# From block 4 to 14 the output's projection of two chunks as seven products of quarters

## The chip, the cores and the metric

The kernel runs on one core of one Trainium2 chip. The metric is the device time of one execution in microseconds (us). Five engines of the core are named as in the profile: PE (matmuls), DVE (VectorE), ACT (ScalarE), POOL (GpSimd) and SP, which here only issues transfers.

## The reference

`x` has 4 sequences of 1024 tokens with 1024 channels. What is computed, cut to its core:

```python
xn = layernorm(x)
h = rmsnorm(xn, qkv_norm_w); q, k, v = split(h @ ternary(qkv_w).T)      # 16 heads of 64
for each chunk of 128 tokens:                                            # S is carried on
    o = D ** -0.5 * ((q k^T * mask) v + (q * lam_t) S)
    S = lam_T * S + (k * lam_rev)^T v
s = rmsnorm(rmsnorm(o, norm_w, 1e-6), proj_norm_w, eps) @ ternary(proj_w).T
g = silu(xn @ ternary(ffn_weight).T + ffn_bias)
out = x + s * g
```

`ternary` rounds a weight matrix to -1, 0 and 1 times one scale, so that the weights are held in 8 bits (fp8) and are exact. The activations are held as two 16-bit parts, a high and a low one (`o_hi`, `o_lo`), and each product with weights is done twice, once for each part, into the same PSUM bank.

## The kernel before

Tokens are taken in chunks of T = 128; two chunks (c = 0, 1) are one block, and there are NB = 16 blocks, four to a sequence. Each engine has its own program, a list of instructions in an order written out by hand, and the engines meet only at semaphores. PE's matmuls write into four PSUM banks of 512 columns, `ring`, which are given out in turn by the list `ring_uses`: the use with number n takes bank n modulo 4, and `free_bank` makes PE wait until the use with number n - 4 has been read out. Four more banks, `att_ps`, serve the attention.

In block i (from block 3 on) PE does in this order:

- four groups of q and k (`project_qk`), with the two small matmuls of the norm of chunk 1 of the block before (`output_scale`, `spread_gamma`) between them;
- k and v of both chunks by `k_product` and `v_product`, and between them the projection of chunk 1 of the block before, `project_out(i - 1, 1, half)`. Here k, v and the ffn are already seven products of quarters instead of eight (Winograd's form of Strassen's scheme: rows are the two chunks, columns the two halves of the channels). A product has 4 x 2 matmuls of 512 columns. The names a11 to a22 are quarters of the activations, S1 to S4 their sums, w11 to w22 quarters of the weights, T1 to T4 their sums; products that share a part of the result share a bank;
- the attention of chunk 0 with products of the ffn between its steps, the same for chunk 1, and then the projection of chunk 0, `project_out(i, 0, half)`.

`project_out` is 8 x 2 matmuls of 512 columns into one bank, four times in a block. DVE makes the operand: `weight_o`, `scale_o` (times the norm's factor, which comes out of PE's `spread_gamma`), ACT's `high_o` rounds it to `o_hi`, DVE's `split_o` subtracts to `o_lo`. DVE's `gate_out` multiplies the bank by the gate, and POOL's `add_out` adds x; SP stores.

In the same stretch DVE prepares the next block: `norm_stats`, `sum_b` and `low_b_sum` for k and v, `low_part` and `sum_y` for the ffn, `add_k` and `add_v`, which add a bank to k or v, and `centre`, which takes mean and deviation off the turned x. POOL's `decay_q` scales q for the carried state; for chunk 0 of a block it is left out where a sequence begins (blocks 0, 4, 8, 12).

Of the kernel before, what the change touches and what calls it, by code (L numbers as in the profile page):

```python
# [36 lines left out]
def program(nc, x, qkv_w, proj_w, decay, ffn_w, ffn_b, norm_cols, x_turned, out):  # L37
# [17 lines left out]
    with ExitStack() as ctx:  # L55
# [16 lines left out]
        xt = sb("xt", [P, 4, C])  # L72
# [21 lines left out]
        arena = sb("arena", [P, ARENA])  # L94
# [28 lines left out]
        k_decay = arena[:, QL_OFF + C:QL_OFF + 2 * C]  # L123
        state = arena[:, ST_OFF:SM_OFF].rearrange("p (k r e) -> p k r e", k=2, r=PR)
# [3 lines left out]
        sq_sum = sb("sq_sum", [P, CHUNKS, 2, T])  # L128
# [6 lines left out]
        s_tok = sb("s_tok", [P, H])  # L135
        s_pair = sb("s_pair", [P, PR])
        cols = sb("cols", [P, 3, NCB])
        peak = sb("peak", [P, 10])
        mean_sq = sb("mean_sq", [P, P])
        neg_magic = sb("neg_magic", [P, 1])  # L140
        to_end = sb("to_end", [P, 1])
        mean_w = sb("mean_w", [P, 1])
        halves = sb("halves", [P, 4])
        wsum = sb("wsum", [P, 5 * NCB])
        wtot = sb("wtot", [P, 4])
# [3 lines left out]
        og = sb("og", [P, 2, 4])  # L149
        diag = sb("diag", [P, CHUNKS, T])  # L150
        sum_cols = sb("sum_cols", [P, PR, 1])
# [5 lines left out]
        diff = sq_sum[:, 0, 0, :]  # L157
        t_row = sq_sum[:, 0, 1, :]
# [60 lines left out]
        s_add_last = sem("last_out_added")  # L219

# [21 lines left out]
        def gate_of(i):  # L242
            return gate_odd if i == 1 else gate_even

# [36 lines left out]
        BY_TOKENS = 3  # L281
        PRODUCTS = ("p1", "p6", "p2", "p7", "p4", "p5", "p3")
# [213 lines left out]
        for i in range(BY_TOKENS, NB):  # L496
            ring_uses += [("qk", i, j) for j in range(CPH)]

            ring_uses += [("proj", i - 1, 1, 0), ("k product", i, "p1"), ("k product", i, "p5"), ("proj", i - 1, 1, 1)]
            ring_uses.append(("k product", i, "p6"))  # L500
# [3 lines left out]
            ring_uses += [("proj", i, 0, 0), ("proj", i, 0, 1)]  # L504
# [22 lines left out]
        def emptied(use):  # L527
# [14 lines left out]
            if kind == "v product":  # L542
                by = {"p1": (s_v, 2 * CHUNKS * HALF + of_pair(use[1], 0)), "p5": (s_vsum, of_pair(use[1], 0)),
                      "p6": (s_v, 2 * CHUNKS * HALF + of_pair(use[1], 1))}
                return by[use[2]]
            if kind == "product":
                return s_z, of_z(use[1], *{"p1": (0, 0), "p6": (1, 0), "p5": (0, 1)}[use[2]])
# [12 lines left out]
            return s_m, of_half(*use[1:])  # L560
# [36 lines left out]
        def tensor_program(pe):  # L597
# [61 lines left out]
            def product(i, name):  # L659
# [18 lines left out]
                for j in range(CPH):  # L678
                    if name == "p4" and i >= BY_TOKENS and j == CPH // 2:
# [1759 lines left out]
```

## Time and profile before

| | |
|---|---|
| median of 3 runs | 1329.47 us (1328.97 to 1329.55) |
| the profiled execution, its own time | 1328.99 us |
| its span in the profile | 1327.8 us |
| PE busy | 1304.3 us, 98% |
| DVE, ACT, POOL busy | 917.4, 581.9, 555.3 us (69%, 44%, 42%) |
| share of PE in the chain that ended last | 95% |

The span leaves out what lies around the program on the device, 1.2 us here. A busy share is that of the whole span; what each engine does in one block is read from a window as long as a block. A matmul is shown with its whole way through the array, so that rows of PE overlap, and the distance from start to start is what one costs.

### The profile page before, as it was taken

The page shows a single profiled execution, that of the slowest core. Times are in us where ns is not written, and L with a number is a line of the kernel's source. Part 1 is how long each engine was busy: PE and PEld are TensorE (multiplying, and loading weights), DVE is VectorE, ACT ScalarE, POOL GpSimd, SP SyncE. Part 2 cuts the span into 40 slices and gives each one's busy share as a digit, 9 for nine tenths or more (in the row PEclk, how much of TensorE's full clock was granted, in tenths as well). Part 3 has the DMA queues.
Part 4 walks back from the last instruction along what each step waited for, and adds up shares of the span by engine and source line. Part 5 has one row for each costly group of instructions (what it writes and reads, how often), then busy time and mean ns, then how long its engine had stood idle before and what let it go on. Part 6 is the DMA issues. An engine that isn't in the chain of part 4 may idle for free.

```text
span 1327.8 us, 25789 instructions
## 1 busy us (share of the span) xinstructions
PE 1304.3 (98%) x10351; PEld 835.2 (63%) x10351; DVE 917.4 (69%) x1457; ACT 581.9 (44%) x1139; POOL 555.3 (42%) x532
## 2 busy tenths in 40 slices
PE   4999999999999999999999999999999999999998
PEld 2577767674666656566674656657566575656655
DVE  7887466786666857667575776857667685766735
ACT  5884144343534544344353434544444453434521
POOL 1432876842433435335331543435334342533332
PEclk9999999999999999999999999999999999999999
DMA  9622201203021030300303021030300203020000
GB/s 363 240 96 65 72 33 42 94 17 120 1 66 71 17 119 18 116 5 17 120 17 120 2 100 37 17 120 17 117 4 20 116 17 120 1 88 18 33 33 33
DMA packets 33432, 90.32 MB, mean 68 GB/s; under 512 B 10529, under 2 KB 10785, under 8 KB 33314
## 3 DMA queue, kind: packets, MB, share of 16 engines
q1 hardware_dynamic: 33024, 88.65, 18.9%
q8 instruction: 83, 1.36, 0.4%
q14 instruction: 35, 0.29, 0.1%
q10 hardware_dynamic: 290, 0.02, 0.0%
HBM read 71.85 MB, written 16.81 MB: 67 GB/s over the span
## 4 chain that ended last, share of the span: by engine, by line
PE 95%; ACT 2%; DVE 1%; DMA 1%; issue 1%; SPq 0%; POOL 0%; ACTq 0%; DVEq 0%; POOLq 0%
PE ring L749 20%; PE ring L879 16%; PE ring L682 13%; PE ring L708 13%; PE ring L734 12%; PE att_ps L786 4%; PE att_ps L836 4%; PE att_ps L832 4%; PE ring L798 2%; PE att_ps L813 2%; PE ring L761 1%; PE ring L655 1%; DMA raw<-in_ffn_w 1%; ACT junk L1698 1%; PE ring L893 1%
## 5 line engine op out<-in xcount | busy, mean ns | idle before, releaser
L749 PE MATMUL ring<-b_lo,qkv_q 128*128 128x256 f16 x1216 | 268.2, 272 | 0.0
L749 PE MATMUL ring<-b_hi,qkv_q 128*128 128x256 f16 x1216 | 268.2, 273 | 0.0
L879 PE MATMUL ring<-proj_q,o_hi 128*128 128x512 fp8e4 x496 | 188.1, 379 | 1.0 <-DVE o_lo L1423 1.0
L879 PE MATMUL ring<-proj_q,o_lo 128*128 128x512 fp8e4 x496 | 188.0, 379 | 0.0
L2140 POOL TENSOR_TENSOR gate_even<-gate_even,bias 128x512 f32<-128x512 f32 x14 | 19.8, 1414 | 275.6 <-ACT gate_even L1817 275.4
L749 PEld LDWEIGHTS ring<-b_hi,qkv_q 128*128 128x128 fp8e4 x1216 | 120.2, 99 | 15.6
L749 PEld LDWEIGHTS ring<-b_lo,qkv_q 128*128 128x128 fp8e4 x1216 | 119.0, 98 | 15.7
L2180 POOL TENSOR_TENSOR sq<-sq,cols 128x1024 f32<-128x1024 f32 x29 | 55.0, 1897 | 157.6 <-DVE b_lo L1255 149.4
L2206 POOL TENSOR_TENSOR xt<-xt,gate_even 128x512 f32<-128x512 f32 x58 | 85.7, 1487 | 81.0 <-DVE gate_even L1440 80.8
L1857 ACT ACTIVATE arena<-ring,wscale 128x512 f32<-128x512 f32 x64 | 44.0, 687 | 128.5 <-PE ring L749 128.5
L1841 ACT ACTIVATE gate_even<-gate_even 128x512 f32<-128x512 f32 x60 | 37.3, 625 | 134.5 <-DVE gate_even L1286 134.5
L836 PE MATMUL att_ps<-arena 128*64 128x128 f32 x1024 | 95.0, 273 | 0.0
L1352 DVE TENSOR_TENSOR arena<-att_ps,mask 128x512 f32<-128x512 f32 x128 | 79.5, 684 | 14.4 <-PE att_ps L786 14.4
L832 PE MATMUL att_ps<-arena 128*64 128x128 f32 x896 | 88.5, 276 | 0.0
L879 PEld LDWEIGHTS ring<-proj_q,o_hi 128*128 128x128 f16 x496 | 48.6, 98 | 58.5 <-DVE o_lo L1423 1.1
L879 PEld LDWEIGHTS ring<-proj_q,o_lo 128*128 128x128 f16 x496 | 48.5, 98 | 56.0
L1286 DVE SCALAR_TENSOR_TENSOR gate_even<-ring,ln,gate_even 128x512 f32<-128x512 f32 x70 | 52.5, 750 | 39.7 <-PE ring L682 39.7
L1440 DVE SCALAR_TENSOR_TENSOR gate_even<-ring,wscale,gate_even 128x512 f32<-128x512 f32 x58 | 43.4, 748 | 45.0 <-PE ring L879 44.6
L2155 POOL TENSOR_TENSOR arena<-arena,lam_q 128x512 f32<-128x512 f32 x56 | 72.8, 1319 | 2.6 <-PE att_ps L836 2.6
L1802 ACT ACTIVATE gate_odd<-ring,wscale 128x512 f32<-128x512 f32 x26 | 17.9, 688 | 122.7 <-PE ring L734 122.7
L2076 POOL TENSOR_TENSOR ln<-ln,halves 128x3 f32<-128x3 f32 x32 | 37.5, 1171 | 80.2 <-DVE ln L1143 79.2
L786 PEld LDWEIGHTS att_ps<-arena 64*128 64x128 f32 x1024 | 59.7, 188 | 13.8 <-issue 13.8
(255 smaller groups left out, 3190.7 us busy)
## 6 DMA issues: line engine op xcount, KB each, us to landing
xt<-in_x SPq DMA_DIRECT2D x62, 512.0 KB, 8.1
out<-xt SPq DMA_DIRECT2D x31, 512.0 KB, 2.7
raw<-in_qkv_w SPq DMA_DIRECT2D x24, 512.0 KB, 15.7
y<-in_x_turned SPq DMA_DIRECT2D x14, 512.0 KB, 6.8
y_odd<-in_x_turned SPq DMA_DIRECT2D x14, 512.0 KB, 7.4
raw<-in_ffn_w SPq DMA_DIRECT2D x8, 512.0 KB, 9.8
norm_rows<-norm_out SPq DMA_DIRECT2D x14, 256.0 KB, 6.0
raw<-in_proj_w SPq DMA_DIRECT2D x6, 512.0 KB, 4.4
```

The source lines that it names most:

```text
L682: ins = pe.matmul(ring[:, b, :], of[:, j, :], weights_of(weights)[:, j, :], start=(begins and j == 0 and k == 0), stop=(j == CPH - 1 and k ...
L708: ins = pe.matmul(ring[:, b, :], of[:, j, :], v_weights_of(weights)[:, j, :], start=(name in ("p1", "p5") and j == 0 and k == 0), stop=(j ...
L734: ins = pe.matmul(ring[:, b, :], of[:, j, :], k_weights_of(weights)[:, j, :], start=(name in ("p1", "p5") and j == 0 and k == 0), stop=(j ...
L749: ins = pe.matmul(ring[:, b, e * BT:(e + 1) * BT], qkv_q[:, cb, o:o + P], part[:, cb, :], start=(cb == 0 and part is b_hi), stop=(cb == NC ...
L786: ins = pe.matmul(att_ps[:, 2 * half + e, j, :], k_t[rows, r, ts], q_t[rows, r, ts], start=True, stop=True)
L832: pe.matmul(att_ps[e * D:(e + 1) * D, half, j, :], state[:, passes_on(g) % 2, r, e * D:(e + 1) * D], q_decay[:, r, :], start=True, stop=Fa ...
L836: ins = pe.matmul(att_ps[e * D:(e + 1) * D, half, j, :], v_tok[:, c, r * P + e * D:r * P + (e + 1) * D], scores_m[:, half, e, j, :], start ...
L879: ins = pe.matmul(ring[:, b, :], part[:, cb, :], proj_q[:, cb, cs], start=(cb == 0 and k == 0), stop=(cb == NCB - 1 and k == 1))
L1352: dve.tensor_tensor(scores_m[:, half, e, :, :], att_ps[:, 2 * half + e, :, :], mask[:, e, half * CPH:(half + 1) * CPH, :], ALU.mult).then_ ...
L2155: pool.tensor_tensor(q_decay[:, hs, :], q_t[:, hs, c * T:(c + 1) * T], lam_q[:, hs, :], ALU.mult).then_inc(s_ql, 1)
L2180: pool.tensor_tensor(sq[:, 0, :, :], sq[:, 0, :, :], over_tokens(cols[:, 1, :], T), ALU.mult).then_inc(s_sqw, 1)
L2206: pool.tensor_tensor(o, o, gate_of(i)[:, c, cs], ALU.add).then_inc(s_add, 1)
```

## The change

1. **The projection by products.** For blocks 4 to 14 (`by_products(i)`) the projection of both chunks is seven products instead of the four `project_out`. p1 and p2 are of chunk 0 alone and stay at the end of block i. The other five are done in block i + 1, between the products of k and v, in the order p6, p7, p5, p4, p3. p6, p7 and p4 add up in one bank (a copy of p1 by ACT begins it), which `ring_uses` holds with the entries "held"; p5 and p3 in another.
2. **Its operands.** `split_o` of chunk 1 goes; DVE makes four sums of quarters (`sum_o`) and five low parts (`low_o_part`), ACT five high parts (`high_o_part`). The weights' sums are made once by POOL, in blocks 3 and 4 (T1, T2, T4, T3), and w12, which T3 overwrites, is restored in block 15.
3. **Its results.** ACT takes two copies of a bank as bases (`begin_out`); DVE's `gate_sum` adds a bank to the base and multiplies by the gate, two instructions where `gate_out` had one. Two of the four parts still go by `gate_out`.
4. **Orders.** In the attention of chunk 1 the ffn's p3 goes ahead, and its p4 goes behind the outputs, next to the projection's p1 (the heading's "p4 behind o"). ACT's `silu(i, 1, 0)` comes last there, POOL's `decay_q(i, 0, .)` comes ahead of its `add_out`s.
5. **x for the norm in one place.** `xt` has three chunks instead of four; the chunk of c = 1 is loaded into the same place as that of c = 0 as soon as `norm_stats` has read it, at the start of the block instead of half a block earlier.

```diff
@@ ring_uses @@
         for i in range(BY_TOKENS, NB):
-            ring_uses += [("qk", i, j) for j in range(CPH)]
-            ring_uses += [("proj", i - 1, 1, 0), ("k product", i, "p1"), ("k product", i, "p5"), ("proj", i - 1, 1, 1)]
-            ring_uses.append(("k product", i, "p6"))
+            if by_products(i - 1):
+                ring_uses += [("qk", i, 0), ("qk", i, 1), ("qk", i, 2), ("held", i - 1, 0), ("qk", i, 3)]
+                ring_uses += [("k product", i, "p1"), ("k product", i, "p5"), ("held", i - 1, 1)]
+                ring_uses += [("k product", i, "p6"), ("o product", i - 1, "p5")]
...
             ring_uses += [("v product", i, "p1"), ("v product", i, "p5"), ("v product", i, "p6")]
@@ emptied @@
+            if kind == "held":
+                return s_m, of_out(use[1], 1, 0)
@@ tensor_program @@
+            def o_product(i, name):
...
+                for j in range(CPH):
+                    for k, of in enumerate(o_part_of(part)):
+                        ins = pe.matmul(ring[:, b, :], of[:, j, :], proj_weights_of(weights)[:, j, :],
+                                        start=(name in ("p1", "p5") and j == 0 and k == 0),
+                                        stop=(j == CPH - 1 and k == 1), skip_group_check=True)
@@ vector_program @@
+            def gate_sum(i, c):
+                n = 2 * (i - BY_PRODUCTS) + (1 if c else 2)
+                base = o_base_of(c)
+                dve.wait_ge(s_ops, of_o_product(i, "p5" if c else "p3"))
...
+                dve.tensor_tensor(gate, gate, base, ALU.mult).then_inc(s_m, 1)
             def gate_out(i, c, half):
-                dve.wait_ge(s_pr, n)
+                if by_products(i):
+                    use = ("o product", i, "p6" if c else "p1")
+                    dve.wait_ge(s_ops, of_o_product(i, "p4" if c else "p2"))
@@ sync_program @@
-                    sync.wait_ge(s_stats, 2 * chunk(i - 1, c) + 1)
-                sync.dma_start(xt[:, c, :], x_rows[row:row + T, :]).then_inc(s_x[c], DMA)
+                    sync.wait_ge(s_stats, 2 * (chunk(i, c) - 1) + 1)
+                sync.dma_start(x_place(i, c), x_rows[row:row + T, :]).then_inc(s_x[c], DMA)
```

The bracket in a row names the semaphores that it waits for. The same rows stand in each block from 5 to 15.

**PE, between the last products of k and v.** Lines L734 and L708 are `k_product` and `v_product` before, L833 and L807 after; L1006 is `o_product`. Before:

```order
L708 MATMUL ring<-qkv_q,b_hi 128x512 [waits k_tokens_made]
...
L734 MATMUL ring<-k_sum_last,b_hi 128x512 [waits k_sum_made]
...
L708 MATMUL ring<-v_sum,b_sum_hi 128x512 [waits k_sum_made,b_sum_lo_made]
...
L708 MATMUL ring<-qkv_q,b_hi 128x512 [waits v_bank_begun]
```

After, the same stretch:

```order
L1006 MATMUL ring<-proj_sum,o_parts 128x512 [waits k_tokens_made,o_part_lo,proj_weights_summed]
...
L807 MATMUL ring<-qkv_q,b_hi 128x512 [waits k_sum_made]
...
L833 MATMUL ring<-k_sum_last,b_hi 128x512 [waits k_sum_made]
...
L1006 MATMUL ring<-proj_sum_last,o_parts 128x512 [waits o_base_made,o_part_lo,proj_weights_summed]
...
L807 MATMUL ring<-v_sum,b_sum_hi 128x512 [waits gated,b_sum_lo_made]
...
L1006 MATMUL ring<-proj_q,o_parts 128x512 [waits o_part_added,o_part_lo]
...
L807 MATMUL ring<-qkv_q,b_hi 128x512 [waits v_bank_begun]
```

The projection's p5, p4 and p3 now stand around v's p1, k's p4 and v's p5. v's p1 waits for `add_k` (k_sum_made) where it waited for ACT's `take_k` (k_tokens_made), and v's p5 waits for DVE's `gate_out` (gated) of the bank that the projection's p4, directly ahead of it, has filled.

**DVE, from `scale_o` of chunk 1 to `add_k`.** Before, L1423 is `split_o`, L1440 `gate_out`, L1239 `add_k`; the rows left out are `norm_stats` and the ffn's parts and sums (L1194, L1210):

```order
L1416 TENSOR_TENSOR ow<-ow,att_ps 128x1024 [waits gamma_spread_ps,o_weighted]
L1194 TENSOR_TENSOR a_lo<-y_odd,a_hi 128x4x128 [waits a_hi_made]
L1210 TENSOR_TENSOR y_odd<-y_odd 128x512 [waits a_lo_made,b_weighed,b_lo_made]
L1423 TENSOR_TENSOR o_lo<-ow,o_hi 128x1024 [waits o_hi_made]
...
L1440 SCALAR_TENSOR_TENSOR gate_even<-ring,wscale,gate_even 128x512 [waits gate_made,proj_ps]
...
L1440 SCALAR_TENSOR_TENSOR gate_even<-ring,wscale,gate_even 128x512 [waits gate_made,proj_ps]
L1239 SCALAR_TENSOR_TENSOR gate_odd<-ring,wscale,gate_odd 128x512 [waits k_base_made,k_tokens_ps] x2
```

After, L1600 is `sum_o`, L1605 `low_o_part`, L1354 `low_part`, L1399 `add_k`, L1613 and L1618 `gate_sum`, L1640 `gate_out`:

```order
L1583 TENSOR_TENSOR ow<-ow,att_ps 128x1024 [waits gamma_spread_ps,o_weighted]
L1600 TENSOR_TENSOR o_row<-arena,ow 128x512 [waits o_scaled,b_sum_lo_made]
L1600 TENSOR_TENSOR ow<-ow 128x512 [waits o_row_summed]
L1600 TENSOR_TENSOR arena<-ow,arena 128x512 [waits o_row_summed]
L1600 TENSOR_TENSOR arena<-arena 128x512 [waits o_row_summed]
L1605 TENSOR_TENSOR o_parts<-ow,o_parts 128x512 [waits o_part_hi]
L1605 TENSOR_TENSOR o_lo<-arena,o_hi 128x512 [waits o_part_hi]
...
L1399 SCALAR_TENSOR_TENSOR gate_odd<-ring,wscale,gate_odd 128x512 [waits k_base_made,k_tokens_ps] x2
L1613 SCALAR_TENSOR_TENSOR ow<-ring,wscale,ow 128x512 [waits o_base_made,o_product_ps]
L1618 TENSOR_TENSOR gate_even<-gate_even,ow 128x512 [waits gate_made,o_part_added]
L1640 SCALAR_TENSOR_TENSOR gate_even<-ring,wscale,gate_even 128x512 [waits gate_made,o_product_ps]
```

Nine instructions of 128x512 take the place of one of 128x1024 ahead of `add_k`, and both `gate_out` of chunk 1 have left that stretch.

**POOL, a block that goes on with a sequence, from the end of the last `norm_scale`.** Before, L2206 is `add_out` and L2155 `decay_q`:

```order
L2078 TENSOR_SCALAR norm_pair<-ln 128x1 [waits ln_pow]
L2079 TENSOR_TENSOR ln<-ln 128x1
L2095 TENSOR_TENSOR ln<-ln,wscale 128x1 [waits ln_amp]
L2206 TENSOR_TENSOR xt<-xt,gate_even 128x512 [waits gated,x_loaded_for_out1] x2
L2155 TENSOR_TENSOR arena<-arena,lam_q 128x512 [waits o_ps_made,q_made] x2
```

After, L2473 is `decay_q` and L2524 `add_out`:

```order
L2379 TENSOR_SCALAR norm_pair<-ln 128x1 [waits ln_pow]
L2380 TENSOR_TENSOR ln<-ln 128x1
L2396 TENSOR_TENSOR ln<-ln,wscale 128x1 [waits ln_amp]
L2473 TENSOR_TENSOR arena<-arena,lam_q 128x512 [waits o_ps_made,q_made] x2
L2524 TENSOR_TENSOR xt<-xt,gate_even 128x512 [waits gated,x_loaded_for_out1] x2
L2524 TENSOR_TENSOR xt<-xt,gate_even 128x512 [waits gated,x_loaded_for_out0]
```

So the two decays now run as soon as the norm's factors are made, in the middle of DVE's sums for the ffn.

## Rows read from the trace of the kernel before

**Rows 1.** Window of block 7; columns: busy us (instructions) by engine, clock, DMA.

```profile
core 0: us, PE busy (x) PEld busy (x) DVE busy (x) ACT busy (x) POOL busy (x), PEclk, DMA share, GB/s
600.93:680.06 79.13, 79.13 (x609) 49.33 (x608) 53.59 (x86) 33.18 (x72) 31.37 (x33) 1.00 0.15 57
```

**Rows 2.** Waits of PE, whole run; columns: us in total, times, longest.

```profile
PE ring L636 <- DVE y L1155: 12.3, 2, 11.6
...
PE ring L879 <- DVE o_lo L1423: 1.0, 1, 1.0
```

**Rows 3.** Timeline of PE, the projection between two products of k in block 7.

```profile
617.00 0.38 PE L879 MATMUL ring<-proj_q,o_hi 128*128 128x512 fp8e4 x1
...
620.23 0.38 PE L879 MATMUL ring<-proj_q,o_lo 128*128 128x512 fp8e4 x1
620.45 0.38 PE L734 MATMUL ring<-k_sum,b_sum_hi 128*128 128x512 fp8e4 x1
```

**Rows 4.** Timeline of DVE, the start of block 7; last column: idle time, releaser.

```profile
604.70 3.94 DVE L1218 TENSOR_TENSOR arena<-arena 128x512 f32<-128x512 f32 x4
...
612.05 1.22 DVE L1416 TENSOR_TENSOR ow<-ow,att_ps 128x1024 f32<-128x1024 f32 x1
613.18 0.69 DVE L1194 TENSOR_TENSOR a_lo<-y_odd,a_hi 128x512 f16<-128x512 f32 x1
...
614.61 1.22 DVE L1423 TENSOR_TENSOR o_lo<-ow,o_hi 128x1024 f16<-128x1024 f32 x1
615.75 1.28 DVE L1135 BATCH_NORM_STATS2 ln<-xt 128x6 f32<-128x512 f32 x2
...
617.57 0.69 DVE L1210 TENSOR_TENSOR y_odd<-y,y_odd 128x512 f32<-128x512 f32 x1
...
620.65 0.75 DVE L1440 SCALAR_TENSOR_TENSOR gate_even<-ring,wscale,gate_even 128x512 f32<-128x512 f32 x1 [0.96 <-PE ring L879]
...
622.10 1.57 DVE L1210 TENSOR_TENSOR y<-y 128x512 f32<-128x512 f32 x1
...
624.80 1.28 DVE L1194 TENSOR_TENSOR sum_lo<-y,sum_hi 128x512 f16<-128x512 f32 x2
...
631.01 0.75 DVE L1239 SCALAR_TENSOR_TENSOR gate_odd<-ring,wscale,gate_odd 128x512 f32<-128x512 f32 x1 [4.27 <-PE ring L734]
```

**Rows 5.** Timeline of POOL, the start of block 7.

```profile
603.50 3.00 POOL L2206 TENSOR_TENSOR xt<-xt,gate_even 128x512 f32<-128x512 f32 x2
...
617.74 1.27 POOL L2076 TENSOR_TENSOR ln<-ln,halves 128x3 f32<-128x3 f32 x1 [4.92 <-DVE ln L1143]
619.10 0.67 POOL L2078 TENSOR_SCALAR norm_pair<-ln 128x1 f32<-128x1 f32 x1
...
621.55 1.58 POOL L2206 TENSOR_TENSOR xt<-xt,gate_even 128x512 f32<-128x512 f32 x1 [1.35 <-DVE gate_even L1440]
...
628.11 2.49 POOL L2155 TENSOR_TENSOR arena<-arena,lam_q 128x512 f32<-128x512 f32 x2
```

**Rows 6.** Timeline of DVE and PE at the end: PE waits for half of a DVE pair.

```profile
1317.08 1.29 DVE L1423 TENSOR_TENSOR b_lo<-ow,b_hi 128x512 f16<-128x512 f32 x2 [0.16 <-ACT b_hi L1896]
...
1317.83 0.39 PE L893 MATMUL ring<-proj_q,b_hi 128*128 128x512 fp8e4 x1 [0.58 <-DVE b_lo L1423]
```

**Rows 7.** Timeline of ACT, the end of block 7 and the start of 8.

```profile
674.80 2.43 ACT L1756 ACTIVATE arena<-y,cols 128x128 f32<-128x128 f32 x8
...
679.47 0.62 ACT L1749 ACTIVATE a_hi<-y_odd 128x512 f16<-128x512 f32 x1
...
683.75 0.69 ACT L1857 ACTIVATE arena<-ring,wscale 128x512 f32<-128x512 f32 x1 [2.62 <-PE ring L749]
```

**Rows 8.** Timeline of DVE, block 7, behind the projection.

```profile
635.21 1.23 DVE L1165 TENSOR_TENSOR y<-y,norm_rows 128x1024 f32<-128x1024 f32 x1 [1.73 <-DMA y<-in_x_turned]
...
645.70 0.75 DVE L1231 SCALAR_TENSOR_TENSOR arena<-ring,wscale,arena 128x512 f32<-128x512 f32 x1 [0.98 <-PE ring L708]
```

**Rows 9.** DMA issues: operation, count, KB each, median us from issue to landing.

```profile
xt<-in_x SPq DMA_DIRECT2D x62, 512.0 KB, 8.1
```

More of the change, by code:

```diff
@@ L872, in project_out @@
                     pe.wait_ge(s_wout, w_n["proj", NCB - 1])
-                pe.wait_ge(s_olo, chunk(i, c) + 1)
+                pe.wait_ge(s_olo, split_whole(chunk(i, c)))
+                if i == NB - 1 and half == 1:
+                    pe.wait_ge(s_pwsum, 5)
                 b = free_bank("proj", i, c, half)
@@ L912, in attention_by_tokens @@
                 outputs(i, c, 1)
+                if by_products(i) and c == 1:
+                    if last:
+                        o_product(i, "p1")
+                        product(i, "p4")
+                    else:
+                        product(i, "p4")
+                        o_product(i, "p1")
+                        update_state(i, 1)
+                    o_product(i, "p2")
+                    return
                 if not last:
@@ L1471, in attention_by_tokens @@
                 begin_z22(i)
+                if by_products(i):
+                    output_scale(i, 0)
+                    end_z22(i)
+                    scale_o(i, 0)
+                    take_z12(i)
+                    split_b(i + 1, 0, 0)
+                    split_o(i, 0)
+                    weight_o(i, 1, 0)
+                    weight_o(i, 1, 1)
+                    split_b(i + 1, 0, 1)
+                    split_b(i + 1, 1, 0)
+                    split_b(i + 1, 1, 1)
+                    take_z21(i)
+                    if not last:
+                        add_state(i, 1)
+                    gate_out(i, 0, 0)
+                    return
                 end_z22(i)
@@ L1659, in vector_program @@
                 scale_o(i - 1, 1)
-                low_part(i, "a22")
-                sum_y(i, "S1")
-                split_o(i - 1, 1)
-                if more:
-                    norm_stats(i + 1, 1)
-                sum_y(i, "S3")
-                low_part(i, "a11")
-                sum_y(i, "S2")
-                gate_out(i - 1, 1, 0)
-                low_part(i, "a12")
-                sum_y(i, "S4")
-                for name in Y_SUMS:
-                    low_part(i, name)
-                gate_out(i - 1, 1, 1)
@@ L2278, in gpsimd_program @@
                     add_out(i - 1, 0, 0)
-                    add_out(i - 1, 0, 1)
+                    if not by_products(i - 1):
+                        add_out(i - 1, 0, 1)
                     if i >= BY_TOKENS:
```

416 lines of the change are left out of this document (339 added, 77 removed).

## The prediction

> **What bounds the kernel now.** I read three views in this order. The waits of PE over the whole run come first: two waits of 12.3 us together at the start, where weights are still loaded, and one of 1.0 us for an `o_lo`, in block 0 [rows 2]. None falls in the steady blocks. Then the window of block 7: PE is busy 79.13 of 79.13 us at a granted clock of 1.00 (the upper of its two levels, 2.4 GHz), DVE 53.59, ACT 33.18, POOL 31.37 [rows 1]. So in this stretch the time is the sum of what PE issues, and each matmul taken out shows in full, as long as nothing new makes PE wait. Last the timelines of one block, for where each engine is when. I give times as block time: the trace's time less 600.93, the start of block 7.
>
> **What is removed.** One projection bank is 16 matmuls from 617.00 to 620.45, 3.45 us, so one costs 0.2156 us [rows 3], and a product of eight 1.725 us. Before there were 64 of them in a block, after there are 7 x 8 = 56: 1.725 us less. Blocks 4 to 14 are 11: 18.97 us less. Nothing is added on PE itself.
>
> **The wait inside the projection.** After the change v's p5 takes the bank in which the projection's p6, p7 and p4 add up, and it stands directly behind p4. In between DVE must do `gate_out` of that bank. What such a round takes is read from three rows. PE's next slot behind the last matmul of a projection is 620.45, and DVE's `gate_out` starts at 620.65: 0.20. It takes 0.75 [rows 3, 4]. Back from DVE to PE: the first half of the pair that begins at 1317.08 and takes 1.29 ends at about 1317.73, and PE, which waited for it, starts at 1317.83: 0.10 [rows 6]. Together 1.05 us, in each of 11 blocks 11.55 us. Bounds: 0.75 alone if both ends overlapped (8.3 us), 1.3 with a colder start of the weight load (14.3 us). DVE is idle there by my reckoning (below), so nothing is added for that. Queued behind v's p5 on PE is the whole rest of the block, so the wait counts in full.
>
> **v's p1 and the chain on DVE.** v's p1 now takes the bank that k's `add_k(i, 0)` reads, and DVE has more to do before that. Block time on DVE, without hindrance:
> - `scale_o` ends at 612.05 + 1.22, that is 12.34, as before, since it hangs on PE's `spread_gamma`.
> - four `sum_o`, each waiting for the one before: the four `sum_b` take 3.94 with POOL's two `add_out` beside them [rows 4, 5]; 0.87 of it is hindrance (below), so 3.07, and 0.1 ahead. 15.5.
> - five low parts at 0.60 (two take 1.28, and the start of the next overlaps), 3.0; `norm_stats` 615.75 to 617.57, 1.82. 20.3.
> - the ffn's parts and sums: before they went from 613.18 to 624.80 + 1.28, 12.90; in that lie `split_o` 1.14, `norm_stats` 1.82, `gate_out` with its idle time 0.96 + 0.67, and 0.87 of hindrance. Left: 7.44. 27.8.
> - `add_k` 0.75. 28.5 [rows 4].
>
> PE comes to v's p1 8 products after the point where the first projection stood (617.00, block time 16.07): k p5, o p6, k p2, k p6, o p7, k p3, k p7, o p5, so at 16.07 + 13.80 = 29.87. The margin is 1.3 us. But POOL's two `decay_q` have been moved ahead of `add_out`. `norm_scale` begins at 617.74 and is through about 0.4 behind 619.10 + 0.67, some 2.5 us after `norm_stats` [rows 5]; with `norm_stats` ending at 18.5 now, the decays begin at 21.0, just as DVE begins the ffn's sums. How they hinder each other is in the trace: the sum y<-y takes 1.57 instead of 0.69, and begins at 622.10 while POOL's `add_out` holds from 621.55 to 623.13 [rows 4, 5]. It ran only when POOL was through: 0.87 for one POOL instruction. Before, the decays stood at 628.11, where DVE waited for PE anyway (4.27 idle before 631.01). Two decays cost DVE 2 x 0.87 = 1.7 up to 2 x 1.25 = 2.5 (2.49 is the pair). With 1.7 `add_k` ends at 30.2 and PE waits 30.3 - 29.87 = 0.5 us; with 2.0 it waits 0.7. I take 0.6. Where a sequence begins there is no decay (blocks 8 and 12), and in block 15 there is no `norm_stats` and the decays come long before. So 8 of the blocks 5 to 15 pay: 4.8 us. Bounds: 0 if the low parts in between do not lock, 10 us if each decay blocks in full.
>
> **What I cost at next to nothing, and what hides it.**
> - Nine `sum_o` and low parts and two more multiplications less `split_o` are some 6.4 us of DVE in a block, five high parts, a bank's copy and two bases less `high_o` some 4 us of ACT. Both engines have room (53.6 and 33.2 of 79) outside the chain above.
> - ACT's silu of the last quarter now waits for the ffn's p4, so `weigh_b` (4.67 us, 674.80 to 679.47) ends some 4.0 us into the next block instead of 0.6 before its start [rows 7]. The next ACT had 2.62 idle ahead of its first q. DVE's `sum_b` begin at 4.1 instead of 3.8 and still end before ACT's high parts of them. Where a sequence has ended it is 5.0, and `spread_gamma` may be late by 0.15, twice.
> - The projection's p2 waits for ACT's copy of p1: 0.2 + 0.59 + 0.1, hidden by `update_state` (1.03) or by the ffn's p4.
> - The projection's p6 at 17.79 needs S2's low part, ready at 16.7; its p7 at 22.97 and p5 at 28.14 have 3 us and more.
> - x for chunk 1 is loaded from 2.2 on, lands some 8.1 us later [rows 9], and is read at 16.7.
> - Behind the projection: `centre` waited for its transfer until 34.3 [rows 8]; `norm_stats` is 1.9 later and `low_part` S4 4 later, so it now begins at about 37, and with POOL's three `add_out` and the state's decay beside it DVE ends `add_v(i, 1)` at some 49.8, when PE wants it for v's p4 at 50.0. No wait, but no room either.
> - w12, T1 to T4 on POOL lie where it is idle. For all of these together, block 15's included, 0.6 us.
>
> **The sum.** -18.97 + 11.55 + 4.8 + 0.6 = -2.0 us. Against the profiled execution's own 1328.99 that is 1327.0; the median shown is 0.48 above that execution, so 1327.5 for the median.
>
> **What the Trainium skill says against it.** The page SBUF — State Buffer, section Who interferes with whom, says that a VectorE instruction with two SBUF inputs contends with a GpSimd instruction that reads SBUF, and that whoever comes second is blocked for the other's whole instruction. The trace agrees in kind (1.57 for 0.69 [rows 4]), and by it the dearer end, two full decays, is the one to expect. That is the last rival below, whose number comes from the rows alone.
>
> **Rivals.**
> - *Only the wait behind p4.* DVE's chain fits into its 1.3 us, because its small parts slip between the decays. For it: the low part at 613.18 and others show 0.69 throughout. Against: POOL's `add_out` shows 1.58, lengthened by DVE's low part ahead of it, so low parts lock as well. 1327.5 - 4.8 = 1322.7.
> - *No wait at all.* If the bank's hand-over behind p4 were hidden, and v's p1 too, 1328.99 + 0.48 - 18.97 = 1310.5. Against it stands the order itself: no PE work lies between p4 and v's p5.
> - *Slower: each decay blocks DVE in full.* 28.5 + 2.5 + 0.1 = 31.1, a wait of 1.25 instead of 0.6 in 8 blocks, +5.2 us: 1332.7. It is slower by more than the 2.7 us below from 1.23 us per decay on. The same locks then eat the 0.2 us that `add_v(i, 1)` has left, and further tenths in each block come on top.
>
> **Chances.** My case 0.52, with a range of its own of 1325 to 1330; only the wait behind p4 0.20; no wait 0.07; slower 0.21. The predicted time is that of the first, 1327.5. The range takes in the second and the last: 1320.5 to 1334. A change of 0.2%, 2.7 us, is about what a measurement of this kernel tells from none. Faster by more than that: a third of my case (0.17) and both faster rivals, 0.44. Within it: 0.35. Slower: 0.21.
>
> **What the trace will show.** If I am right, PE's waits name `gate_out` behind the projection's p4 eleven times with about 1.05 us and `add_k` ahead of v's p1 some eight times with 0.5 to 0.8, and DVE's ffn sums show two of some 1.6 in those blocks. I am wrong if v's p5 starts without a gap, if v's p1 waits in blocks 8 and 12 too (then the chain itself is longer than 28.5), or if v's p4 or the scores wait for DVE, which would be the pile-up behind `centre`.

## The result, and the profile after

| | before | after |
|---|---|---|
| median | 1329.22 us, 6 runs (1328.44 to 1329.69) | 1333.70 us, 6 runs (1333.01 to 1334.43) |
| ratio, 95% interval | | 1.0035 (1.0022 to 1.0047) |
| span of the profiled execution | 1327.8 us | 1332.4 us |

The changed kernel is slower by 4.5 us. I had forecast 1327.5, and slower with a chance of 0.21. The number lies in the range, but the sign is wrong.

The page of the kernel after, busy times and the chain that ended last:

```profile
PE 1293.3 (97%) x10263; PEld 823.1 (62%) x10263; DVE 1015.5 (76%) x1567; ACT 617.5 (46%) x1216; POOL 603.8 (45%) x537
...
PE 79%; DVE 13%; POOL 3%; issue 2%; ACT 2%; DMA 1%; SPq 0%; DVEq 0%; POOLq 0%; ACTq 0%
```

PE is busy 11.0 us less than before, as work was taken out; yet the chain, 95% PE before, now runs through DVE and POOL for 16%. The waits of PE over the whole run, with the columns of [rows 2], to which they answer:

```profile
PE ring L735 <- DVE y L1315: 12.4, 2, 11.6
PE ring L807 <- DVE gate_even L1640: 10.3, 11, 0.9
PE ring L807 <- DVE gate_odd L1399: 3.0, 8, 0.4
...
PE att_ps L958 <- POOL sq_sum L2507: 1.8, 3, 0.6
...
PE att_ps L967 <- POOL diag L2517: 0.6, 3, 0.2
```

The first was there before. The second and third are the two waits of the forecast; the last two, both for POOL, were in no term of it. A wait in this view counts only the time in which PE is empty. What it costs is read from start to start (start of the waiting matmul less start of the one ahead, less 0.2156), about 0.15 more each time. The window of block 7, with the columns of [rows 1], where it is 79.13 us with PE busy throughout:

```profile
599.58:678.76 79.18, 77.87 (x602) 48.31 (x601) 63.17 (x96) 36.18 (x77) 32.86 (x32) 1.00 0.18 58
```

The block is as long as before; the product that it no longer does was given back as waits. The granted clock is 1.00 in both, the upper level. The distances between the starts of blocks, from the first matmul of each, give the whole account:

| block | before, us | after, us | product(s) fewer | lost in it |
|---|---|---|---|---|
| 4 | 78.31 | 76.41 | -3.45 (two) | 1.55 |
| 5, 6, 9, 10, 13, 14 | 80.06 | 80.36 | -1.73 | 2.03 each |
| 7, 11 | 79.13 | 79.18 | -1.73 | 1.78 each |
| 8, 12 | 78.31 | 79.23 | -1.73 | 2.65 each |
| 15 and the end | 91.71 | 94.53 | +1.73 (five for four) | 1.10 |

The two waits of the forecast, in block 7. Timeline of PE after, at v's p1, then at the projection's p4 and v's p5:

```profile
630.00 0.39 PE L807 MATMUL ring<-qkv_q,b_hi 128*128 128x512 fp8e4 x1 [0.38 <-DVE gate_odd L1399]
...
633.46 1.89 PE L1006 MATMUL ring<-proj_sum_last,o_parts 128*128 128x512 fp8e4 x8
636.28 0.38 PE L807 MATMUL ring<-v_sum,b_sum_hi 128*128 128x512 fp8e4 x1 [0.94 <-DVE gate_even L1640]
```

Timeline of DVE after, from the ffn's sums to `gate_out`, and of POOL in the same stretch:

```profile
621.19 1.78 DVE L1370 TENSOR_TENSOR y_odd<-y,y_odd 128x512 f32<-128x512 f32 x1
622.89 1.75 DVE L1354 TENSOR_TENSOR a_lo<-y,a_hi 128x512 f16<-128x512 f32 x1
...
629.19 1.40 DVE L1399 SCALAR_TENSOR_TENSOR gate_odd<-ring,wscale,gate_odd 128x512 f32<-128x512 f32 x2
...
635.39 0.75 DVE L1640 SCALAR_TENSOR_TENSOR gate_even<-ring,wscale,gate_even 128x512 f32<-128x512 f32 x1 [3.41 <-PE ring L1006]
```

```profile
621.16 2.94 POOL L2473 TENSOR_TENSOR arena<-arena,lam_q 128x512 f32<-128x512 f32 x2
```

The projection's p4 starts at 633.46 and v's p5 2.82 behind it instead of 1.725: 1.10 lost. DVE had been idle for 3.41 us, so this is the round through one bank and nothing else. At v's p1 PE waits until the first `add_k` has ended; the two instructions of DVE that begin at 621.19 and 622.89 take 1.78 and 1.75 instead of 0.69, beside POOL's two decays from 621.16 to 624.10. The Trainium skill, page SBUF — State Buffer, section Who interferes with whom, says that the second to come is blocked for the whole instruction of the other; these rows agree nearly: DVE lost 1.09 and 1.06 us, a little less than the 1.25 that a decay takes in the pair of [rows 5].

What I had not priced is at the norm of chunk 0. The first block of a sequence, block 8: POOL after, then PE after.

```profile
736.29 2.50 POOL L2473 TENSOR_TENSOR arena<-arena,lam_q 128x512 f32<-128x512 f32 x2
...
742.94 0.45 POOL L2507 TENSOR_TENSOR sq_sum<-sq 128x128 f32<-128x128 f32 x1
```

```profile
742.55 0.38 PE L781 MATMUL ring<-ffn_sum,sum_lo 128*128 128x512 fp8e4 x1
743.53 0.35 PE L958 MATMUL att_ps<-small,sq_sum 128*128 128x1 f32 x2 [0.61 <-POOL sq_sum L2507]
```

`output_scale(i, 0)` has moved from behind the ffn's p7 to behind its p5, and in blocks 4, 8 and 12 POOL's chain of decays and squares is not done by then. In block 7 the same matmul waits for the last masked scores of DVE, which no wait in the view shows. DVE and PE after, then PE before:

```profile
663.37 2.48 DVE L1515 TENSOR_TENSOR arena<-att_ps,mask 128x512 f32<-128x512 f32 x4 [0.35 <-PE att_ps L886]
...
665.67 0.38 PE L781 MATMUL ring<-ffn_sum,sum_lo 128*128 128x512 fp8e4 x1
665.91 0.38 PE L958 MATMUL att_ps<-small,sq_sum 128*128 128x1 f32 x2
666.15 0.38 PE L781 MATMUL ring<-ffn_q,a_hi 128*128 128x512 fp8e4 x1
```

```profile
665.38 0.38 PE L682 MATMUL ring<-ffn_q,a_lo 128*128 128x512 fp8e4 x1
665.59 0.28 PE L858 MATMUL att_ps<-mean_w,sq_sum 128*128 128x1 f32 x2
665.73 0.38 PE L682 MATMUL ring<-ffn_q,sum_hi 128*128 128x512 fp8e4 x1
```

The masks end at 663.37 + 2.48 = 665.85 and the matmul starts at 665.91. From the product's last matmul to the next one's first it is 0.48 us after and 0.35 before: 0.13 in each block.

### The profile page after: what moved, and what is told of

Same layout as the page of the kernel before. It is cut to its first block, busy times and chain, and to the rows that moved or that the text cites. A ratio compares the mean times of both kernels' runs of the same rounds, so it can differ in the third digit from the quotient of the medians.

```text
span 1332.4 us, 25917 instructions
## 1 busy us (share of the span) xinstructions
PE 1293.3 (97%) x10263; PEld 823.1 (62%) x10263; DVE 1015.5 (76%) x1567; ACT 617.5 (46%) x1216; POOL 603.8 (45%) x537
## 4 chain that ended last, share of the span: by engine, by line
PE 79%; DVE 13%; POOL 3%; issue 2%; ACT 2%; DMA 1%; SPq 0%; DVEq 0%; POOLq 0%; ACTq 0%
PE ring L848 18%; PE ring L807 13%; PE ring L781 11%; PE ring L1006 7%; PE ring L833 6%; PE ring L982 5%; PE att_ps L886 4%; PE att_ps L932 4%; PE att_ps L936 4%; DVE a_lo L1354 2%; PE ring L898 2%; PE att_ps L913 2%; DVE y_odd L1370 1%; PE ring L861 1%; DVE sum_lo L1354 1%
## 5 line engine op out<-in xcount | busy, mean ns | idle before, releaser
L2524 POOL TENSOR_TENSOR xt<-xt,gate_even 128x512 f32<-128x512 f32 x58 | 93.5, 1615 | 179.5 <-DVE gate_even L1618 133.4
L2377 POOL TENSOR_TENSOR ln<-ln,small 128x3 f32<-128x3 f32 x32 | 37.3, 1167 | 100.3 <-DVE ln L1303 99.3
L2473 POOL TENSOR_TENSOR arena<-arena,lam_q 128x512 f32<-128x512 f32 x56 | 76.8, 1390 | 9.8 <-ACT arena L2102 7.0
L1640 DVE SCALAR_TENSOR_TENSOR gate_even<-ring,wscale,gate_even 128x512 f32<-128x512 f32 x36 | 27.0, 750 | 56.7 <-PE ring L1006 42.3
L2485 POOL TENSOR_TENSOR arena<-arena,lam_T 64x512 f32<-64x512 f32 x48 | 62.2, 1296 | 13.4 <-DVE arena L1557 11.5
L886 PE MATMUL att_ps<-arena 64*128 64x128 f32 x1024 | 65.8, 278 | 0.5 <-ACT sq L2128 0.5
L936 PEld LDWEIGHTS att_ps<-arena 128*64 128x64 f32 x1024 | 63.5, 137 | 0.8 <-issue 0.7
L781 PE MATMUL ring<-ffn_q,a_lo 128*128 128x512 fp8e4 x168 | 63.6, 379 | 0.0
```

Of the source, the lines that this page charges most:

```text
L781: ins = pe.matmul(ring[:, b, :], of[:, j, :], weights_of(weights)[:, j, :], start=(begins and j == 0 and k == 0), stop=(j == CPH - 1 and k ...
L886: ins = pe.matmul(att_ps[:, 2 * half + e, j, :], k_t[rows, r, ts], q_t[rows, r, ts], start=True, stop=True)
L936: ins = pe.matmul(att_ps[e * D:(e + 1) * D, half, j, :], v_tok[:, c, r * P + e * D:r * P + (e + 1) * D], scores_m[:, half, e, j, :], start ...
L2473: pool.tensor_tensor(q_decay[:, hs, :], q_t[:, hs, c * T:(c + 1) * T], lam_q[:, hs, :], ALU.mult).then_inc(s_ql, 1)
L2524: pool.tensor_tensor(o, o, gate_of(i)[:, c, cs], ALU.add).then_inc(s_add, 1)
```

## The experiments

All are timed against the kernel before (median 1329.08 or 1329.09). Where nothing else is said, an edit is one to the changed kernel, 1333.7.

**1. The projection's p3 ahead of v's p5.**

```diff
@@ tensor_program @@
                     o_product(i - 1, "p4")
-                    v_product(i, "p5")
                     o_product(i - 1, "p3")
+                    v_product(i, "p5")
```

> Edit: the projection's p3 is issued ahead of v's p5, so that 1.725 us of PE work lies between p4 and the bank that v's p5 takes. Theory (the wait behind p4 is a real loss of 1.10 us, eleven times, and 0.2 + 0.75 + 0.1 fits under one product): the wait for gate_even at v's p5 is gone, 1333.7 - 12.1 = 1321.6, ratio to before 0.9943. Rival (DVE is behind at that place, and would be late one product later for the operand of the projection's p3 or for v's p4): the wait only moves, and less than 3 us are gained, 1331 or more. Rival 2 (a matmul that starts in a bank just read costs PE something whenever): half is gained, about 1327.5.

Measured: 1321.59 us, ratio 0.9947 (0.9934 to 0.9959). The wait for `gate_even` is gone from the view, and the eleven rounds were worth 12.1 us, the whole. Swapping two lines turns the change from a loss into a gain. PE after p4, in block 7:

```profile
631.81 1.89 PE L1006 MATMUL ring<-proj_sum_last,o_parts 128*128 128x512 fp8e4 x8
633.53 1.89 PE L1006 MATMUL ring<-proj_q,o_parts 128*128 128x512 fp8e4 x8
635.26 0.38 PE L807 MATMUL ring<-v_sum,b_sum_hi 128*128 128x512 fp8e4 x1
```

No gap: the round of 1.10 us fits under the 1.725 of one product.

**2. POOL's decays behind the three `add_out` again, and 3. both edits.**

```diff
@@ gpsimd_program @@
-                        decay_q(i, 0, 0)
-                        decay_q(i, 0, 1)
                         add_out(i - 1, 1, 1)
                         add_out(i - 1, 1, 0)
                         add_out(i - 1, 0, 1)
+                        decay_q(i, 0, 0)
+                        decay_q(i, 0, 1)
```

> Edit: POOL's two decays of q for chunk 0 go behind the three add_out again, as they stood before the change. Theory (the wait of v's p1 for add_k comes from DVE being held for about 2.1 us by the two decays): the wait for gate_odd falls from 8 times 0.54 us to at most two hundredths, DVE's sums for the ffn take 0.69 again, 1333.7 - 4.3 = 1329.4, ratio 1.0002. The decays then stand beside centre and add_v, where DVE may be late for v's p4; if so up to 2 us come back. Rival (DVE's chain is too long by itself, with nine instructions in the place of one): the wait stays above 0.3 us in 8 blocks and appears in blocks 8 and 12 as it does not now; gain under 2 us, 1332 or more.

> Both edits: the projection's p3 ahead of v's p5, and POOL's decays behind the add_outs. Theory (two independent waits): they add up, 1333.7 - 12.1 - 4.3 = 1317.3, ratio 0.9911. Rival (without the two waits PE comes 1.6 us earlier to v's p4, for which DVE's centre and add_v were just in time by my count of 0.2 us): a third wait opens for add_v or the scores, of up to 1 us in each block, 1322 to 1326.

Measured: 1329.37 us for the decays alone, ratio 1.0002 (0.9993 to 1.0011), as expected; no wait for `gate_odd` is left, so DVE's chain as such is short enough. Both together 1320.67 us, ratio 0.9941 (0.9928 to 0.9953), 3.4 us short of the sum of the two: the third wait of the rival, though smaller than its 1322 to 1326. Of the run with both, a row of PE's waits, then DVE and PE in block 7:

```profile
PE ring L807 <- DVE arena L1391: 3.3, 8, 0.8
```

```profile
641.02 3.42 DVE L1524 TENSOR_TENSOR gate_odd<-gate_odd,lam_k 128x512 f32<-128x512 f32 x2
644.37 1.40 DVE L1391 SCALAR_TENSOR_TENSOR arena<-ring,wscale,arena 128x512 f32<-128x512 f32 x2
```

```profile
645.83 0.39 PE L807 MATMUL ring<-v_sum_last,b_hi 128*128 128x512 fp8e4 x1 [0.37 <-DVE arena L1391]
```

The decays now stand beside `centre`, `decay_k_tokens` and `add_v`, and v's p4 waits for `add_v` (3.9 us from start to start, in the same eight blocks). The wait of v's p1 was not removed but handed on, to the place of which the prediction said that it had no room.

**4. The decays where both engines are idle.** With experiment 1, POOL's order is `add_out(i - 1, 1, 1)`, the two decays, `add_out(i - 1, 1, 0)`.

```diff
@@ gpsimd_program @@
-                        decay_q(i, 0, 0)
-                        decay_q(i, 0, 1)
                         add_out(i - 1, 1, 1)
+                        decay_q(i, 0, 0)
+                        decay_q(i, 0, 1)
                         add_out(i - 1, 1, 0)
```

> Edits: the projection's p3 ahead of v's p5, and POOL's two decays between its first and its second add_out, where in the run with both edits DVE stood idle for 3.7 us (behind gate_sum, until the bank of the projection's p4 is full) and POOL for 3.2. Theory (what v's p1 and v's p4 wait for is DVE held by POOL's instructions; the decays cost nothing where DVE is idle): neither the wait of v's p1 for add_k nor that of v's p4 for add_v is left, 1317 us, ratio 0.9909. Rival (DVE's work between centre and add_v is too long for PE without the decays too): the wait of v's p4 stays, about 0.3 to 0.5 in 8 blocks, 1320 to 1321.

Measured: 1317.63 us, ratio 0.9915 (0.9902 to 0.9929), as the theory has it. POOL in block 7, and DVE with the idle time that holds it:

```profile
629.76 1.26 POOL L2524 TENSOR_TENSOR xt<-xt,gate_even 128x512 f32<-128x512 f32 x1 [10.09 <-DVE gate_even L1618]
630.98 2.49 POOL L2473 TENSOR_TENSOR arena<-arena,lam_q 128x512 f32<-128x512 f32 x2
634.22 2.11 POOL L2524 TENSOR_TENSOR xt<-xt,gate_even 128x512 f32<-128x512 f32 x1 [0.75 <-DVE gate_even L1640]
```

```profile
628.93 0.69 DVE L1618 TENSOR_TENSOR gate_even<-gate_even,ow 128x512 f32<-128x512 f32 x1
633.32 0.75 DVE L1640 SCALAR_TENSOR_TENSOR gate_even<-ring,wscale,gate_even 128x512 f32<-128x512 f32 x1 [3.70 <-PE ring L1006]
```

Both decays end at 633.47, DVE had nothing to do from 629.62 to 633.32, and neither v's p1 nor v's p4 waits in block 7.

**5. The early decays in the kernel before.**

```diff
@@ gpsimd_program @@
+                    if i > BY_TOKENS + 1:
+                        decay_q(i, 0, 0)
+                        decay_q(i, 0, 1)
                     add_out(i - 1, 1, 0)
...
                     add_out(i - 1, 1, 1)
-                    decay_q(i, 0, 0)
-                    decay_q(i, 0, 1)
+                    if i <= BY_TOKENS + 1:
+                        decay_q(i, 0, 0)
+                        decay_q(i, 0, 1)
```

> The kernel before, with one part of the change alone: from block 5 on POOL's two decays of q for chunk 0 stand ahead of the two add_out of chunk 1 instead of behind them. Theory (the decays hold DVE, but this costs time only where DVE's chain has no slack, and before DVE waited 4.27 us ahead of add_k): some DVE instructions between block time 19 and 23 take 1.5 us and more, add_k is not late, and the time is that of the kernel before, 1329.1, ratio 1.0000. Rival (the early decays cost by themselves): +0.5 in 8 blocks, 1333, ratio 1.003.

Measured: 1329.10 us, ratio 1.0001 (0.9992 to 1.0010). DVE in block 7 of it:

```profile
622.85 1.57 DVE L1210 TENSOR_TENSOR y<-y 128x512 f32<-128x512 f32 x1
624.34 1.75 DVE L1194 TENSOR_TENSOR sum_lo<-y_odd,sum_hi 128x512 f16<-128x512 f32 x1
...
631.75 0.75 DVE L1239 SCALAR_TENSOR_TENSOR gate_odd<-ring,wscale,gate_odd 128x512 f32<-128x512 f32 x1 [3.19 <-PE ring L734]
```

DVE loses a microsecond more to POOL than it did in the kernel before (the 1.57 stood there too [rows 4], the 1.75 is new), its idle time ahead of `add_k` falls from 4.27 [rows 4] to 3.19, and PE sees nothing of it. That is half of what DVE loses in the changed kernel, but twice as much would have fitted into the 4.27 too. The hindrance costs time only with a longer chain on DVE.

**6. From block 12 on only.**

```diff
-        BY_PRODUCTS = 4
+        BY_PRODUCTS = 12
```

> Edit: the change begins at block 12 instead of block 4 (one number), so only blocks 12, 13 and 14 have their projection by products, and block 15 takes over the last five of them. All else stays: one place for x, the weights' sums. Theory (the loss is made in the blocks themselves, with the pitches of the trace after against before: block 12 -1.9 as block 4, blocks 13 and 14 +0.3 each, block 15 and the rest +2.8): 1329.2 + 1.5 = 1330.7, ratio 1.0011. Rival (a fixed cost outside the projection: x in one place, the weights' sums on POOL): the loss stays near the whole 4.5 us, 1333.5, ratio 1.0033. By the sum of my forecast alone (-1.725 a block, +1.05, +0.6 where decays are) it would be about -0.5, 1328.7.

Measured: 1330.62 us, ratio 1.0013 (1.0004 to 1.0022), where the sum of the blocks says 1330.7. Before block 12 all distances are those of the kernel before. So x in one place and one chunk less cost nothing, and neither do the weights' sums, which POOL makes here in blocks 11 and 12.

**7. POOL's order in the first block of a sequence.**

```diff
@@ gpsimd_program @@
+                early = by_products(i) and is_first(chunk(i, 0))
-                if c == 1:
+                if c == 1 and not early:
                     sum_squares(i, 0)
...
-                if not is_first(g) and not is_last(g):
+                if not is_first(g) and not is_last(g) and not (early and c == 1):
                     decay_state(i, c)
...
                     decay_q(i, 1, 0)
+                    if early:
+                        sum_squares(i, 0)
                     decay_q(i, 1, 1)
...
                         output_scale(i, 0)
+                    if early:
+                        decay_state(i, 1)
```

> Edit, in blocks 4, 8 and 12 alone: POOL's sum_squares(i, 0) stands between its two decays for chunk 1 and decay_state(i, 1) behind output_scale(i, 0), so that the sum is ready about 1.2 us earlier and the diagonal about 2 us. Theory (PE's 0.74 and 0.35 us at the two small matmuls of the norm in the first block of a sequence are a wait for POOL's chain of decays, squares and decayed state): 1333.7 - 3.2 = 1330.5, ratio 1.0010. Rival (the decay of the second half of q, or the state's, comes late instead, and the outputs wait for it): no gain, 1333 to 1334.

Measured: 1330.67 us, ratio 1.0012 (1.0003 to 1.0020). Block 8 takes 78.06 us instead of 79.23, block 4 75.24 instead of 76.41, and both waits for POOL are gone. The sum is now ready at 741.09 + 0.45:

```profile
735.47 1.27 POOL L2473 TENSOR_TENSOR arena<-arena,lam_q 128x512 f32<-128x512 f32 x1
...
741.09 0.45 POOL L2507 TENSOR_TENSOR sq_sum<-sq 128x128 f32<-128x128 f32 x1
```

**8. `update_state` ahead of the last products.**

```diff
@@ tensor_program @@
-                        product(i, "p4")
-                        o_product(i, "p1")
                         update_state(i, 1)
+                        o_product(i, "p1")
+                        product(i, "p4")
                     o_product(i, "p2")
```

> Edit, in the nine blocks that pass a state on within a sequence: behind the outputs come update_state, the projection's p1, the ffn's p4, the projection's p2, where it was p4, p1, update_state, p2. Theory (a change between fp8 products and fp32 matmuls costs PE some 0.1 us, and update_state in the middle of the products makes two more of them): -0.17 in 9 blocks, 1332.2, ratio 1.0023. Rival (the ffn's p4 is 2.75 us later, and ACT's silu and weigh_b behind it were just in time): q and k of the next block or the norm's matmuls wait, 0.5 us a block or more, 1336 or more.

Measured: 1331.48 us, ratio 1.0017 (1.0009 to 1.0026), 2.2 us less than after. The nine blocks are shorter by 0.26 each (80.10 for 80.36), more than the 0.17 that I had read. PE at the end of block 6, after, and then in this run:

```profile
592.88 0.39 PE L936 MATMUL att_ps<-arena 128*64 128x128 f32 x4
593.20 0.39 PE L781 MATMUL ring<-ffn_sum,a_hi 128*128 128x512 fp8e4 x1
...
596.45 0.38 PE L1006 MATMUL ring<-proj_q,o_lo 128*128 128x512 fp8e4 x1
596.76 1.15 PE L913 MATMUL att_ps<-arena,gate_odd 128*64 128x64 f32 x32
597.84 0.39 PE L1006 MATMUL ring<-proj_q,o_hi 128*128 128x512 fp8e4 x1
```

```profile
592.65 0.39 PE L936 MATMUL att_ps<-arena 128*64 128x128 f32 x4
592.87 1.10 PE L913 MATMUL att_ps<-arena,gate_odd 128*64 128x64 f32 x32
593.90 0.39 PE L1006 MATMUL ring<-proj_q,o_hi 128*128 128x512 fp8e4 x1
```

From the outputs' last row to the product it is 0.32 from start to start, where it is 0.22 to `update_state` (592.65 to 592.87); from the product to `update_state` it is 0.31, where two fp8 matmuls follow at 0.22; `update_state` itself takes 1.08 instead of 1.03. The ffn's p4, 2.75 us later, made nothing late.

**9. The same in the kernel before, the other way round.** DVE's `add_state` goes behind its `split_b` in these blocks.

```diff
@@ tensor_program @@
-                if not last:
+                between = c == 1 and 4 <= i < NB - 1
+                if not last and not between:
                     update_state(i, c)
...
                     project_out(i, 0, 0)
+                    if not last and between:
+                        update_state(i, c)
```

> The kernel before, with update_state(i, 1) between the two banks of the projection of chunk 0 in the nine blocks from 4 to 14 that pass a state on within a sequence (and DVE's add_state behind its split_b, so that it holds nothing up). Theory (each further change from fp8 products to fp32 matmuls and back costs PE about 0.26 us, as in the experiment that took it away from the changed kernel): +0.26 in nine blocks, 1329.1 + 2.3 = 1331.4, ratio 1.0018. Rival (the 0.26 us of that experiment came from the order of p4, p1 and p2 in it, a hand-over of banks, and not from the change of type): no change, 1329.1, ratio 1.0000.

Measured: 1331.26 us, ratio 1.0017 (1.0008 to 1.0026). The blocks take 80.32 instead of 80.06, and block 7, which passes no state on, 79.13 as before. So the 0.26 is the place of `update_state`, and nothing of the products.

My two expectations put it down to the change between fp8 and fp32. The trace of before shows that the type alone doesn't make it. The norm's fp32 matmuls, whose weights fill the array (128*128 in their row), follow an fp8 one at 0.21 (665.38 to 665.59 above), what an fp8 matmul costs among its own kind; the two of them and the step back to fp8 take 0.14 (to 665.73). And between two fp32 groups a tenth is lost where the weights go from 128*128 to 128*64. PE before, in block 7:

```profile
651.04 1.04 PE L798 MATMUL ring<-ident,gate_odd 128*128 128x128 f32 x8
652.01 0.44 PE L832 MATMUL att_ps<-arena 128*64 128x128 f32 x4
```

The eight start 0.109 apart, so the last starts at 651.80; the next row is 0.20 behind it. `update_state` and the outputs have weights of 128*64, the products of 128*128. So what goes with the loss in all these rows is the change between weights that fill the array and weights that fill half of it.

**10. The norm's matmuls 0.86 us later.**

```diff
@@ tensor_program @@
-                    if name == ("p3" if by_products(i) else "p4") and i >= BY_TOKENS and j == CPH // 2:
+                    if name == "p7" and by_products(i) and j == CPH // 2:
+                        output_scale(i, 0)
+                    if name == "p4" and not by_products(i) and i >= BY_TOKENS and j == CPH // 2:
                         spread_gamma(i, 0)
...
                     product(i, "p5")
-                    output_scale(i, 0)
                     product(i, "p7")
                     product(i, "p3")
+                    spread_gamma(i, 0)
```

> Edit: output_scale(i, 0) goes from behind the ffn's p5 into the middle of its p7, 0.86 us later, and spread_gamma(i, 0) from the middle of p3 to its end, also 0.86 later. Theory (PE waits at the first for the masked scores of DVE, 0.14 us in 11 blocks, and for POOL's sum, 0.74 us in 3, and at the second for POOL's diagonal, 0.35 us in 3; each of these is ready within 0.86 us): 1333.7 - 1.5 - 2.2 - 1.1 = 1328.9, and with one fp8 to fp32 change less in each block perhaps 1 us less again, ratio 0.9990 to 0.9998. Rival (the norm's factor comes 0.86 us later to DVE, so that scale_o, the rounding on ACT and the low part are late for the projection's p1): a wait of up to 0.8 us in 11 blocks, 1330 to 1337.

Measured: 1333.01 us, ratio 1.0028 (1.0017 to 1.0039): mixed. Ordinary blocks are 0.14 shorter (80.22 for 80.36), and the matmul pair of the norm follows at 0.35 again, so that wait was real; nothing came of the change from fp8 to fp32 that the edit saves, and the norm's weights are 128*128, as the products' are. But in blocks 7 and 11, where the projection's p1 stands directly behind the outputs, the low part comes late:

```profile
673.21 0.39 PE L1008 MATMUL ring<-proj_q,o_hi 128*128 128x512 fp8e4 x1 [0.59 <-DVE o_lo L1591]
```

These blocks take 79.79 instead of 79.18, as the rival has it. Nor did the waits for POOL's diagonal all go: 0.3 us of it is left in blocks 4, 8 and 12, and in 8 and 12 `spread_gamma` for the block before now waits 0.54.

**11. Four edits, and 12. five.** The first has experiments 1, 4, 7 and 8 together, the second also 10, in the nine blocks alone that don't end a sequence.

> The changed kernel with four edits together: the projection's p3 ahead of v's p5; POOL's decays of q between its first and second add_out; POOL's sum_squares and decay_state in another order in blocks 4, 8, 12; update_state ahead of the last products in nine blocks. Theory (four independent losses): 1317.6 - 1.18 x 3 - 0.26 x 9 = 1311.7, ratio 0.9870. Rival (PE 0.3 to 1.2 us earlier in a block finds the next producer late, as with the first two edits together): one more wait, 1313 to 1316.

> As the version with four edits, and output_scale(i, 0) in the middle of the ffn's p7 with spread_gamma(i, 0) behind p3, but only in the nine blocks that don't end a sequence, since in the two that do the low part was late for the projection's p1 by 0.66 us. Theory (the 0.14 us that PE waits there for the masked scores is gone in nine blocks, and update_state stands ahead of the projection's p1 and covers the later factor): 1311.7 - 1.3 = 1310.4, ratio 0.9860. Rival (the factor's way through DVE, POOL and ACT is late for p1 here too): up to 0.6 in some blocks, 1311.7 or more.

Measured: 1312.00 us, ratio 0.9873 (0.9859 to 0.9886), and 1311.95 us, ratio 0.9871 (0.9857 to 0.9884). With four edits an ordinary block takes 78.46 us; 80.06 less one product is 78.34, and the 0.12 between is the wait for the masks. The chain that ended last in the run with four:

```profile
PE 94%; ACT 2%; DVE 2%; DMA 1%; issue 1%; SPq 0%; POOL 0%; ACTq 0%; DVEq 0%; POOLq 0%
```

The fifth takes that wait out too (78.33), but v's p4 waits for `add_v` in block 7 (77.92 for 77.53); the medians don't tell the two versions apart. Either is 17 us faster than the kernel before, near the 1310.5 of the rival without any wait. In block 6 v's p4 waits 0.40 us for `add_v` in both, and just so in experiments 1 and 4. The traces show what it hangs on: `centre` is held up by its transfer. DVE stands idle for `y<-in_x_turned` for 0.95 us in block 6 with four edits and for 0.21 in block 7 with five, and not at all in block 5. Why the transfer lands late there stays open.

## Why the prediction was wrong

Its steps one by one, in us over the whole run; the last column is start to start from the trace of after, or from the experiment named.

| term | forecast | measured |
|---|---|---|
| eleven products fewer | -18.97 | -18.97 (the span of experiment 12 is 18.0 below before) |
| v's p5 behind the projection's p4 | 11.55 | 12.09, eleven times 1.10 |
| v's p1 for `add_k` | 4.8 | 4.29, eight times 0.54 |
| the norm's two matmuls wait for POOL, blocks 4, 8, 12 | 0 | 3.5, three times 1.17 (experiment 7; 0.74 and 0.35 at the two matmuls themselves) |
| the norm's first matmul waits for the masks | 0 | 1.4, eleven times 0.13 (experiment 10) |
| `update_state` between products | 0 | 2.3, nine times 0.26 (experiments 8, 9) |
| all small things together | 0.6 | nothing else seen |
| sum | -2.0 | +4.6; the spans differ by 4.6 |

**Right:** what bounds the kernel, the price of a product, both large waits with their place, number and nearly their size, and the blocks without the second (8, 12, 15). The round through a bank, put together from three rows as 1.05, was 1.10. DVE's chain ended where it was reckoned: without decays the first `add_k` ends at block time 28.2 (I had 28.5), the two decays take 1.09 and 1.06 (between my 0.87 and 1.25). That they, and not the longer chain alone, make the wait is shown by experiments 2 and 4; that it takes both, by experiment 5.

**Wrong: the step "for all of these together, block 15's included, 0.6 us".** It was 7.2. In two places something had been moved on PE, and I had costed neither. The rows that I should have read, all before: POOL and PE in block 8, DVE in block 7.

```profile
741.41 0.46 POOL L2189 TENSOR_TENSOR sq_sum<-sq 128x128 f32<-128x128 f32 x1
```

```profile
742.97 0.28 PE L858 MATMUL att_ps<-mean_w,sq_sum 128*128 128x1 f32 x2
```

```profile
661.35 2.48 DVE L1352 TENSOR_TENSOR arena<-att_ps,mask 128x512 f32<-128x512 f32 x4 [0.35 <-PE att_ps L786]
```

- `output_scale(i, 0)` one product earlier. The change to PE's program shows it, and what it waits for was in the trace of before: POOL's sum ends at 741.87, and PE wanted it at 742.97. A margin of 1.1 us can't bear a step of 1.725; what remains, 0.6, is what the view of the waits shows (0.74 from start to start). Nor did I look at the masks, which end at 661.35 + 2.48 = 663.83, 1.76 ahead of PE's 665.59: the step of 1.725 and the 0.06 from DVE to PE use that up.
- "Nothing is added on PE itself". The number of matmuls fell as I said, but their order costs too: `update_state`, with weights of half the array, between two products, 0.26.

**The rival that each decay blocks DVE in full** forecast 1332.7, close to what was measured, but it isn't what happened: it needed a wait of 1.25 at v's p1, and there is one of 0.54. The nearness is chance. The rival "only the wait behind p4" fell with the 0.54, and "no wait at all" came true only after the orders had been mended.

The remark on `add_v` ("no wait, but no room either") was right twice over: no wait in the kernel after, and one of 3.9 us in all as soon as experiment 3 took PE's other waits away (0.4 of it, in block 6, with experiment 1 already).

## What to carry to other kernels

Where PE is the bound, list every instruction that the change moves on it, the one-column matmuls too, and read for each from the trace of before when its operand was ready and when PE wanted it: a margin smaller than the shift is a wait. Between the last matmul into a bank and the first of the bank's next use put a product of other work; here exchanging two lines was worth 12 us. Of two engines that hold each other up, put the movable instruction where the other is idle: at either end of its freedom it made a wait, in the gap none.

## What the runs showed of the hardware

- A change between matmuls with weights of 128*128 and of 128*64, in either direction, costs PE some 0.1 us from start to start: 0.31 and 0.32 for 0.22 around `update_state`, and 0.20 for 0.11 between two fp32 groups (experiment 9). A change between fp8 and fp32 with both at 128*128 costs nothing that the rows show (0.21 behind an fp8 matmul, as between two of them). A state update of 32 matmuls of 128*64 costs 0.26 more between two products than next to the outputs, and the same in the two kernels (experiments 8 and 9). What in PE makes it, no run here shows.
- A wait can be paid without being seen: 0.13 us at the norm's matmul stands in no row of the waits, since the row of the matmul ahead of it (665.67 + 0.38) ends only after the waiting one has begun (665.91). Only distances from start to start, or between the starts of blocks, show it.
